# An adaptive-layer-norm block with a 4-bit gated network: the up product's first pass through seven block products as well

## The chip, the cores and the metric

The kernel runs on one core of a Trainium2 chip. The metric is the device time of one execution in microseconds, the median of three runs. Five engines run their own instruction streams in program order and meet through semaphores: TensorE (PE in the views), VectorE (DVE), ScalarE (ACT), GpSimd (POOL, idle here but for the start) and SyncE (SP), which issues every DMA.

## What is computed

```python
mod = (_silu(L0_c) @ L0_wmod).reshape(L0_c.shape[0], 6, 1, -1)      # sa, ca, ga, sb, cb, gb
h = _layernorm(x, axis=-1) * (1 + ca) + sa
x = x + ga * _L0_attn_ref(h, ...)          # h @ (masked 1024x1024 weight).T
h = _layernorm(x, axis=-1) * (1 + cb) + sb
x = x + gb * _L0_ffn_ref(h, ...)
# ffn: w1, w2 (2752x1024) and w3 (1024x2752) are 4-bit codes through a 16-entry table, times a scale per 64
h = jax.nn.silu(jnp.einsum('bsd,hd->bsh', x, w1)) * jnp.einsum('bsd,hd->bsh', x, w2)
return jnp.einsum('bsh,dh->bsd', h, w3)
```

x is 4 batches of 512 tokens by 1024, all float32. Two of the batches are called pass 0 here and the other two pass 1.

## The kernel before

**Numbers.** Each float32 operand of a product is split into a high and a low part (`_hi`, `_lo`, both in the format fp32r), and a product is three matmuls: high by high, high by low, low by high. Splitting costs a copy (the high part) and a subtraction (the low part). A 4-bit code becomes a weight in 8 chained Prelu activations on ACT (`lines`) and one multiplication with the scale on DVE.

**Stages.** First comes the attention product with both layer norms. Then the up product: hidden width 2752 is 21 tiles of 128 (numbered 0 to 20) and a half tile (FULL, 21). A tile has a gate part from w1 (w = 0) and an up part from w2 (w = 1). Then the down product, which is not changed here.

**Pass 0** is plain: `up_group(c, w, b)` is, for tile c, part w and batch b, 8 chunks of the inner dimension by 3 matmuls, so 24 matmuls of 128x128 by 512 columns into one of six PSUM banks, 96 for a tile. ACT does the `silu` of the w = 0 groups, DVE multiplies the two into h (`make_h`), SP stores h. Beside it ACT decodes tile c + 1 (`lines`, once for each w), DVE scales and splits it (`finish`), and DVE also forms five sums of halves of w1 and w2 (`sums`) which SP stores into the DRAM tensor `t_d`, for pass 1.

**Pass 1** computes the 2x2 blocks (gate and up, by batch) with seven block products in place of eight, each of 12 matmuls, 84 for a tile. The weight operands m1 to m7 come back from `t_d` (`load_stream`), are split again (`stream_high` on ACT, `stream_low` on DVE), and each product has a PSUM bank of its own. Sums and differences of the two batches' inputs (`x_add`, `x_high`, `x_low`) are made once, the last of them while pass 0 still runs. DVE adds the products up (`use_m1` to `use_m7`). ACT decodes w3 beside it.

**Order.** Nothing is scheduled by a program: each engine's list of calls is written out by hand, and an engine does exactly the next call, or waits. `load_codes` brings a tile's codes by DMA into a place that an earlier tile's raw weights held.

## Time and profile before

| | us |
|---|---|
| median of three runs | 1570.31 (1570.2 to 1570.99) |
| span of the profiled execution | 1567.6 |
| around the span, against the median | 2.7 |
| PE busy | 1539.4 |
| DVE busy | 1029.5 |
| ACT busy | 989.6 |

The span is from the first to the last instruction of one profiled execution. PE is the TensorE matmul stream. A single matmul is shown with 0.39 us since it is pipelined; how often one starts is read from the starts in the timeline.

### The profile page before, as it was taken

Reading aid. Unit: us, or ns where it says so; the run is one execution under the profiler, and the core shown is the slowest. Engines: PE = TensorE matmul, PEld = TensorE weight load, DVE = VectorE, ACT = ScalarE, POOL = GpSimd, SP = SyncE. Lnnn points to the kernel's source line nnn. Section 1 sums busy time; section 2 is a strip of 40 time slices with the busy share of each in tenths; the row PEclk is TensorE's granted clock in tenths of the full one; section 3 lists DMA queues with packets and bytes.
Section 4 is the critical chain, followed back from the end, with each engine's and each line's share of the span. In section 5 each row is a group of like instructions: output and inputs, shape, how many; then the busy total and the mean of one; then the engine's idle time right before and its main releaser. Section 6 shows DMA issues by size and latency. Waiting matters only on the chain.

```text
span 1567.6 us, 19154 instructions
## 1 busy us (share of the span) xinstructions
PE 1539.4 (98%) x7200; PEld 1269.6 (81%) x7200; DVE 1029.5 (66%) x1486; ACT 989.6 (63%) x1290; POOL 5.5 (0%) x10
## 2 busy tenths in 40 slices
PE   5899999999999999999999999999999999999999
PEld 3688888888888888888888888888888888888887
DVE  5687786555555455547676666666875757956994
ACT  3475676998888888884898988785433432333220
POOL 0000000000000000000000000000000000000000
PEclk9999999999999999999999999999999999999999
DMA  9976423564555445532778787786777868947973
GB/s 368 372 258 228 134 81 138 177 200 166 186 169 187 153 162 180 178 128 97 257 228 252 207 250 208 207 254 171 260 292 272 332 204 302 343 160 268 397 279 122
DMA packets 170139, 345.97 MB, mean 221 GB/s; under 512 B 14752, under 2 KB 65344, under 8 KB 170048
## 3 DMA queue, kind: packets, MB, share of 16 engines
q1 hardware_dynamic: 170048, 344.76, 65.1%
q8 instruction: 57, 0.93, 0.3%
q14 instruction: 34, 0.28, 0.1%
HBM read 249.77 MB, written 94.93 MB: 220 GB/s over the span
## 4 chain that ended last, share of the span: by engine, by line
PE 96%; DMA 2%; DVE 0%; ACT 0%; SPq 0%; issue 0%
PE ps L1916 10%; PE ps L1915 10%; PE ps L1914 10%; PE ps L1988 9%; PE ps L1987 9%; PE ps L1989 9%; PE ps L1925 9%; PE ps L1927 9%; PE ps L1926 9%; PE ps L1832 4%; PE ps L1834 4%; PE ps L1833 4%; DMA wmod<-wmod 2%; PE ps L1789 2%; PE ps L1772 1%; DVE attn_w_lo L1368 0%
## 5 line engine op out<-in xcount | busy, mean ns | idle before, releaser
L861 ACT ACTIVATE w_raw<-w_raw 128x1024 f32<-128x1024 f32 x287 | 304.6, 1061 | 9.1
L1914 PE MATMUL ps<-ffn_in_hi,w_hi 128*128 128x512 f32 x688 | 268.6, 390 | 0.0
L1916 PE MATMUL ps<-ffn_in_hi,w_lo 128*128 128x512 f32 x688 | 267.8, 389 | 0.0
L1915 PE MATMUL ps<-ffn_in_lo,w_hi 128*128 128x512 f32 x688 | 267.7, 389 | 0.0
L1987 PE MATMUL ps<-t_hi,s_hi 128*128 128x512 f32 x616 | 239.6, 389 | 0.0
L1988 PE MATMUL ps<-t_lo,s_hi 128*128 128x512 f32 x616 | 239.6, 389 | 0.0
L1989 PE MATMUL ps<-t_hi,s_lo 128*128 128x512 f32 x616 | 239.6, 389 | 0.0
L1925 PE MATMUL ps<-x_m_hi,stream_hi 128*128 128x512 f32 x604 | 235.0, 389 | 0.0
L1926 PE MATMUL ps<-x_m_lo,stream_hi 128*128 128x512 f32 x604 | 235.0, 389 | 0.0
L1927 PE MATMUL ps<-x_m_hi,stream_lo 128*128 128x512 f32 x604 | 235.0, 389 | 0.0
L1114 ACT ACTIVATE s_hi<-s_raw 128x1408 fp32r<-128x1408 f32 x56 | 77.4, 1383 | 241.2 <-DVE s_raw L1624 192.6
L873 ACT ACTIVATE w_raw<-w_raw 128x1024 f32<-128x1024 f32 (+1 forms) x154 | 163.4, 1061 | 4.4
L1172 DVE SCALAR_TENSOR_TENSOR w_raw<-w_raw,w_scale 128x1024 f32<-128x1024 f32 x41 | 50.3, 1226 | 174.4 <-ACT w_raw L861 174.4
L1916 PEld LDWEIGHTS ps<-ffn_in_hi,w_lo 128*128 128x128 f32 x688 | 129.1, 188 | 26.8
L1915 PEld LDWEIGHTS ps<-ffn_in_lo,w_hi 128*128 128x128 f32 x688 | 129.2, 188 | 26.6
L1914 PEld LDWEIGHTS ps<-ffn_in_hi,w_hi 128*128 128x128 f32 x688 | 129.2, 188 | 26.5
L1987 PEld LDWEIGHTS ps<-t_hi,s_hi 128*128 128x128 f32 x616 | 115.6, 188 | 24.1
L1989 PEld LDWEIGHTS ps<-t_hi,s_lo 128*128 128x128 f32 x616 | 115.6, 188 | 24.0
L1988 PEld LDWEIGHTS ps<-t_lo,s_hi 128*128 128x128 f32 x616 | 115.6, 188 | 23.9
L1927 PEld LDWEIGHTS ps<-x_m_hi,stream_lo 128*128 128x128 f32 x604 | 113.4, 188 | 23.6
L1926 PEld LDWEIGHTS ps<-x_m_lo,stream_hi 128*128 128x128 f32 x604 | 113.4, 188 | 23.6
L1925 PEld LDWEIGHTS ps<-x_m_hi,stream_hi 128*128 128x128 f32 x604 | 113.4, 188 | 23.4
(136 smaller groups left out, 2078.1 us busy)
## 6 DMA issues: line engine op xcount, KB each, us to landing
s_raw<-h_d SPq DMA_DIRECT2D x96, 704.0 KB, 5.6
stream_raw<-t_d SPq DMA_DIRECT2D x150, 256.0 KB, 3.4
t_d<-combined SPq DMA_DIRECT2D x106, 256.0 KB, 2.6
wmod<-wmod SPq DMA_DIRECT2D x12, 2048.0 KB, 15.3
t_raw<-w_d SPq DMA_DIRECT2D x88, 256.0 KB, 6.1
w_codes<-w12q SPq DMA_DIRECT2D x41, 512.0 KB, 5.3
h_d<-h_tile SPq DMA_DIRECT2D x44, 256.0 KB, 2.4
h_d<-up_c SPq DMA_DIRECT2D x44, 256.0 KB, 3.3
```

What stands on the lines that cost most here:

```text
L861: act.activation(RAWF[r], RAWF[r] if j else RQ[r][:], ACT.Prelu, bias=bias, scale=sign, alpha=slope).then_inc(line_ready, 1)
L873: act.activation(E3[p][0:rows, :], (E3 if j else E3Q)[p][0:rows, :], ACT.Prelu, bias=bias, scale=sign, alpha=slope).then_inc(w3_line, 1)
L1114: act.activation(SH[p][:], SR[p][:, 1], ACT.Copy).then_inc(s_hi, 1)
L1914: pe.matmul(acc, RH[r][:, k, :], HH[:, b, k, :], start=(k == 0), stop=False)
L1915: pe.matmul(acc, RH[r][:, k, :], HL[:, b, k, :], start=False, stop=False)
L1916: last = pe.matmul(acc, RL[r][:, k, :], HH[:, b, k, :], start=False, stop=(k == C - 1))
L1925: pe.matmul(acc, th[:, k, :], xh[:, k, :], start=(first and k == 0), stop=False)
L1926: pe.matmul(acc, th[:, k, :], xl[:, k, :], start=False, stop=False)
L1927: last = pe.matmul(acc, tl[:, k, :], xh[:, k, :], start=False, stop=(stop and k == HALF_C - 1))
L1987: pe.matmul(acc, SH[p][:, k, :], TH[place(i)][k][:], start=(k == 0), stop=False)
L1988: pe.matmul(acc, SH[p][:, k, :], TL[place(i)][k][:], start=False, stop=False)
L1989: last = pe.matmul(acc, SL[p][:, k, :], TH[place(i)][k][:], start=False, stop=(k == HC - 1))
```

## The change

Only tiles 0 to 2 of pass 0 stay plain (`PLAIN = 3`). Tiles 3 to 20 of pass 0 go through the seven block products too. A step g is one tile of one pass; g = 0 is tile 3 of pass 0, and g = 18 the first tile of pass 1.

- Products of a step now share three PSUM banks: m1, m2 and m5 open them, m4 goes onto m2's bank, m3 onto m5's, m7 and m6 onto the same two. They go onto a bank only when ACT or DVE has read what is in it: m4 waits for ACT's copy of m2, m3 for DVE's use of m5, m7 for the copy of m2 + m4, m6 for the silu of m5 + m3. m7 and m6 of a step come after m1, m2 and m5 of the next.
- Block weights have twelve places in SBUF, taken in turn. In pass 0 DVE writes the sums straight into them (`weight_sum`), and makes high and low parts (`split_up`); SP stores the sums to `t_d` out of them, and a low part, which takes the sum's place, waits for that store.
- The inputs of the ffn product go through a DRAM tensor `xm_d`: `store_modulated` after each tile of 128 tokens, `load_stage` as four pieces of 1 MB a pass. `x_sum`, `x_high` and `x_low` now exist for both passes. ACT's and DVE's next write of the modulated tile waits for the store of the one before.
- `lines(n)` decodes both parts of a tile in one activation of 128x2048, and is one tile further ahead.
- The transposes of pass 1's inputs move from plain tiles 1 to 8 to the steps of tiles 4 to 11.

The core of the diff:

```diff
+    PLAIN = 3
+    GROUPS = [(c, w, b) for c in range(PLAIN) for w, b in order0(c)]
...
+    OPEN, CLOSE, MIDDLE = ("m1", "m2", "m5"), ("m7", "m6"), ("m4", "m3")
+    STEPS_UP = [(0, c) for c in range(PLAIN, FULL)] + [(1, c) for c in range(FULL)]
+    LAST_STEP = [FULL - PLAIN - 1, len(STEPS_UP) - 1]
+    TAILS = [-1, -2]
     TAIL_PARTS = [("m2", "m2", 0), ("m4", "m4", 0), ("m2", "m5", 1), ("m3", "m3", 1)]
...
+    UP_PRODUCTS = with_ends(
+        lambda g: [(g, n) for n in OPEN] + [(g - 1, n) for n in CLOSE if has_previous(g)] + [(g, n) for n in MIDDLE],
+        lambda g, tail: [(tail, 0), (tail, 1), (g, "m7"), (g, "m6"), (tail, 2), (tail, 3)])
...
+    def up_bank(g, name):
+        return 2 + 3 * (g % 2) + {"m5": 0, "m3": 0, "m6": 0, "m2": 1, "m4": 1, "m7": 1, "m1": 2}[name]
...
+                    old = n - 2
+                    if old < PLAIN:
+                        sp.wait_ge(w12_lo, 2 * old + 2)
+                        sp.wait_ge(ts_added, len(SUM_NAMES) * (old + 1))
+                    else:
+                        sp.wait_ge(t_ready, READY.index((step_of(0, old), "m3" if w == 0 else "m4")) + 1)
+                        sp.wait_ge(sum_made, UP_SUMS.index((step_of(0, old), "m6")) + 1)
...
+            def store_modulated(e):
+                b, k = place2(e)
+                sp.wait_ge(modulated2, e + 1)
+                if e >= SHARED_FROM:
+                    sp.wait_ge(half_modulated, e - SHARED_FROM + 1)
+                for d in range(2):
+                    row = (2 * b + d) * P
+                    sp.dma_start(xm_d[row:row + P, :].rearrange("p (c t) -> p c t", c=HALF_C)[:, :, k * P:(k + 1) * P],
+                                 HM[hm_of(e)][:, HALF_C * d:HALF_C * (d + 1), :]).then_inc(xm_stored[hm_of(e)], 16)
+
+            def load_stage(pas, d, b):
+                row = (2 * (2 * pas + b) + d) * P
...
+            store_modulated(6)
             sp.wait_ge(gated, TILES)
             for w in range(2):
                 load_s12(1, w)
+            for w in range(2):
+                load_codes(2, w)
+            sp.wait_ge(xm_stored[1], xm_stores(6))
+            for d in range(2):
+                load_stage(0, d, 0)
+            for w in range(2):
+                store_part(0, w, w)
+            store_modulated(HALF_TILES - 1)
+            sp.wait_ge(xm_stored[1], xm_stores(HALF_TILES - 1))
+            for d in (1, 0):
+                load_stage(0, d, 1)
+            for name in SUM_NAMES:
+                store_sum(0, name)
+            for n in range(1, PLAIN):
+                for w in range(2):
+                    store_part(n, w, w)
+                    load_s12(n + 1, w)
+                for name in SUM_NAMES:
+                    store_sum(n, name)
+                if n == 2:
+                    load_codes(3, 0)
+                    load_codes(3, 1)
+                for b in range(2):
...
+            for d, b in ((0, 1), (1, 1), (0, 0), (1, 0)):
+                if (d, b) == (0, 0):
+                    sp.wait_ge(sum_made, len(UP_SUMS))
...
+                load_stage(1, d, b)
...
-            def lines(n, w, first=0, last=NL):
-
-                r, J = ring(n, w), job(n, w)
-                act.wait_ge(codes_loaded[r], 16 * ((n + 1) // 2))
+            def lines(n, first=0, last=NL):
+
+                cols = slice(0, C * P * (1 if n == FULL else 2))
+                act.wait_ge(codes_loaded[n % 2], code_loads(n))
...
-                        act.wait_ge(line_ready, NL * J + j)
-                    act.activation(RAWF[r], RAWF[r] if j else RQ[r][:], ACT.Prelu,
+                        act.wait_ge(line_ready, NL * (n - 1) + j)
+                    act.activation(RAW2[n % 2][:, cols], RAW2[n % 2][:, cols] if j else RQ2[n % 2][:, cols], ACT.Prelu,
                                    bias=bias, scale=sign, alpha=slope).then_inc(line_ready, 1)
...
+                        act.wait_ge(xm_stored[1], xm_stores(e - 1))
...
+            lines(1, 2)
+            silu(0, 0)
+            lines(2, 0, 3)
+            silu(0, 1)
+            lines(2, 3)
+            silu(1, 0)
+            for name in ("m1", "m4", "m3"):
+                x_high(0, name)
+            silu(1, 1)
+            lines(3)
+            silu(2, 0)
+            lines(4, 0, 3)
+            silu(2, 1)
+            lines(4, 3, 5)
+            x_high(0, "m7")
+            x_high(0, "m6")
+            lines(4, 5)
+            for c in range(PLAIN, FULL):
+                g, n = step_of(0, c), c + 2
+                if has_previous(g):
+                    copy_up(g - 1, "m4")
+                    silu_up(g - 1, 1)
+                if n <= FULL:
+                    lines(n, 0, 2)
+                copy_up(g, "m2")
+                if n <= FULL:
+                    lines(n, 2, 5)
+                if turned_in(c) is not None:
+                    input2(turned_in(c))
+                if has_previous(g):
+                    silu_up(g - 1, 0)
+                if n <= FULL:
+                    lines(n, 5)
+            g, tail = LAST_STEP[0], TAILS[0]
+            copy_up(g, "m4")
+            silu_up(g, 1)
+            x_high(1, "m1")
+            silu_up(tail, 0)
+            x_high(1, "m2")
+            silu_up(g, 0)
+            x_high(1, "m5")
+            x_high(1, "m4")
+            for name in OPEN:
+                weight_high_up(step_of(1, 0), name)
+            silu_up(tail, 1)
+            x_high(1, "m3")
+            for c in range(FULL):
...
+            def split_up(g, names):
+                for name in names:
+                    if (g, name) not in ACT_HI:
+                        weight_high_up(g, name)
+                for name in names:
+                    weight_low_up(g, name)
...
+            sums(0)
+            make_h(0, 0)
+            finish(1, 0)
+            finish(1, 1)
+            sums(1)
+            make_h(0, 1)
+            for name in ("m1", "m4", "m3", "m6", "m7"):
+                x_sum(0, name)
+            finish(2, 0)
+            finish(2, 1)
+            sums(2)
+            make_h(1, 0)
+            x_low(0, "m1")
+            make_h(1, 1)
+            x_low(0, "m4")
+            x_low(0, "m3")
+            combine(3, 0)
+            combine(3, 1)
+            for name in OPEN:
+                weight_sum(0, name)
+            split_up(0, OPEN + ("m4",))
+            make_h(2, 0)
+            make_h(2, 1)
+            split_up(0, ("m3",))
+            for name in CLOSE:
+                weight_sum(0, name)
+            x_low(0, "m7")
+            x_low(0, "m6")
+            split_up(0, CLOSE)
+            for c in range(PLAIN, FULL):
+                g, n = step_of(0, c), c + 1
+                nxt = step_of(0, n)
+                if n == FULL:
+                    combine(FULL, 0)
+                    weight_sum(nxt, "m2")
+                else:
+                    combine(n, 0)
+                    combine(n, 1)
+                    for name in OPEN + CLOSE:
+                        weight_sum(nxt, name)
+                    split_up(nxt, OPEN)
+                both_used(g)
+                first_left(g)
+                if turned_in(c) is not None:
+                    modulate_half(turned_in(c))
+                if has_previous(g):
+                    finish_c11(g - 1)
+                split_up(nxt, ("m4",))
+                if has_previous(g):
+                    finish_c22(g - 1)
+                split_up(nxt, ("m3",))
+                if has_previous(g):
+                    make_h_up(g - 1, 1)
+                split_up(nxt, ("m2",) if n == FULL else CLOSE)
+                if has_previous(g):
+                    make_h_up(g - 1, 0)
+
+            gl, tail, first = LAST_STEP[0], TAILS[0], step_of(1, 0)
+            x_sum(1, "m1")
+            x_low(1, "m1")
+            x_low(1, "m2")
+            finish_c11(gl)
+            make_h_up(tail, 0)
+            finish_c22(gl)
+            make_h_up(gl, 1)
+            make_h_up(gl, 0)
+            x_low(1, "m5")
+            x_sum(1, "m4")
+            split_up(first, OPEN)
+            make_h_up(tail, 1)
+            x_low(1, "m4")
+            x_sum(1, "m3")
             def w3_combine(j):
                 p, rows = j % 3, w3_rows(j)
                 dve.wait_ge(w3_line, NL * (j + 1))
@@ -1590,31 +1872,35 @@
...
+                elif name == "m4":
+                    pe.wait_ge(up_copied, 2 * g + 1)
+                elif name == "m3":
+                    pe.wait_ge(up_c_step, c_at(g, "e"))
+                elif name == "m7":
+                    pe.wait_ge(up_copied, 2 * g + 2)
+                elif name == "m6":
+                    pe.wait_ge(silu_done, gated_by(g, 1))
+                block_product(ps[:, up_bank(g, name), :], TT[slot_of(g, name)], x_operand(g, name), name in OPEN, True, name not in OPEN)
...
```

The first place is DVE between the first and the second plain tile. `w_raw` are decoded weights, `combined` the sums for pass 1, `h_tile` is h, `x_m_raw` a sum of two input blocks. Before:

```order
L1172 SCALAR_TENSOR_TENSOR w_raw_89<-w_raw_89,w_scale_93 128x1024 [waits s12_loaded_1,line_ready]
L1177 CAST w_hi_73<-w_raw_89 128x1024 [waits combined]
L1179 TENSOR_TENSOR w_lo_77<-w_raw_89,w_hi_73 128x1024 [waits w12_hi]
L1193 TENSOR_TENSOR combined_101<-w_raw_89 128x512
L1459 TENSOR_TENSOR h_tile_96<-silu_g_94,ps 128x512 [waits group_done,silu_done]
L1193 TENSOR_TENSOR combined_102<-w_raw_88,w_raw_89 128x512
L1193 TENSOR_TENSOR combined_103<-w_raw_89,w_raw_88 128x512
L1459 TENSOR_TENSOR h_tile_97<-silu_g_95,ps 128x512 [waits group_done,silu_done]
L1193 TENSOR_TENSOR combined_100<-w_raw_88,w_raw_89 128x512 [waits ts_stored_0]
L1172 SCALAR_TENSOR_TENSOR w_raw_86<-w_raw_86,w_scale_92 128x1024 [waits s12_loaded_0,line_ready]
L1177 CAST w_hi_70<-w_raw_86 128x1024 [waits combined,group_done]
L1179 TENSOR_TENSOR w_lo_74<-w_raw_86,w_hi_70 128x1024 [waits w12_hi]
```

After:

```order
L1742 TENSOR_TENSOR x_m_raw<-ffn_in_raw_00_153,ffn_in_raw_11_156 128x2048 [waits stage_loaded_11,stage_loaded_00]
L1742 TENSOR_TENSOR x_m_raw<-ffn_in_raw_10_154,ffn_in_raw_00_153 128x2048 [waits stage_loaded_00,stage_loaded_10]
L1742 TENSOR_TENSOR x_m_raw<-ffn_in_raw_01_155,ffn_in_raw_11_156 128x2048 [waits stage_loaded_11,stage_loaded_01]
L1742 TENSOR_TENSOR ffn_in_raw_01_155<-ffn_in_raw_00_153,ffn_in_raw_01_155 128x2048 [waits xs_added,stage_loaded_01,stage_loaded_00]
L1742 TENSOR_TENSOR ffn_in_raw_11_156<-ffn_in_raw_10_154,ffn_in_raw_11_156 128x2048 [waits xs_added,stage_loaded_11,stage_loaded_10]
L1379 SCALAR_TENSOR_TENSOR w_raw_80<-w_raw_80,w_scale_84 128x1024 [waits s12_loaded_0,line_ready]
L1388 CAST w_hi_66<-w_raw_80 128x1024 [waits combined,group_done]
L1390 TENSOR_TENSOR w_lo_70<-w_raw_80,w_hi_66 128x1024 [waits w12_hi]
L1379 SCALAR_TENSOR_TENSOR w_raw_80<-w_raw_80,w_scale_85 128x1024 [waits s12_loaded_1,line_ready]
L1388 CAST w_hi_67<-w_raw_80 128x1024 [waits combined,group_done]
L1390 TENSOR_TENSOR w_lo_71<-w_raw_80,w_hi_67 128x1024 [waits w12_hi]
L1410 TENSOR_TENSOR combined_94<-w_raw_80 128x512 [waits ts_stored_2,combined]
```

The five sums of inputs now stand ahead of the scaling and splitting of tile 2 (rows with `w_scale`), which the third plain tile on PE waits for.

The second place is SP between the sums of two tiles; `w_codes` are the DMAs that bring codes. Before:

```order
L587 DMA t_d<-combined_102 128x512 [waits ts_added]
L587 DMA t_d<-combined_103 128x512 [waits ts_added]
L594 DMA h_d<-h_tile_97 128x4x128 [waits h_made]
L587 DMA t_d<-combined_100 128x512 [waits ts_added]
L463 DMA w_codes_84<-w12q 128x1024 [waits pure_stored_2,ts_added,w12_lo]
L463 DMA w_codes_85<-w12q 128x1024 [waits pure_stored_3,ts_added,w12_lo]
L469 DMA w_scale_92<-w12s 128x1x128 [waits combined]
L582 DMA t_d<-w_raw_86 128x512 [waits combined]
```

After:

```order
L711 DMA t_d<-w_raw_80 128x512 [waits combined]
L580 DMA w_scale_85<-w12s 128x1x128 [waits combined]
L717 DMA t_d<-combined_94 128x512 [waits ts_added]
L717 DMA t_d<-combined_95 128x512 [waits ts_added]
L717 DMA t_d<-combined_92 128x512 [waits ts_added]
L717 DMA t_d<-combined_93 128x512 [waits ts_added]
L717 DMA t_d<-combined_94 128x512 [waits ts_added]
L574 DMA w_codes_79<-w12q 128x1024 [waits pure_stored_2,ts_added,w12_lo]
L574 DMA w_codes_79<-w12q 128x1024 [waits pure_stored_3,ts_added,w12_lo]
L736 DMA h_d<-h_tile_88 128x4x128 [waits h_made]
L736 DMA h_d<-h_tile_89 128x4x128 [waits h_made]
```

The codes of tile 3 (`w_codes_79`, before `w_codes_84` and `_85`) are now issued behind the last stored sum of tile 2; before, behind the last of tile 1.

The third place is DVE at the end of pass 0. `up_left_then_c` and `up_c` are results of the block products, `up_weight_lo` the low parts of pass 1's first weights; before, `stream_lo` are those. Before:

```order
L1464 TENSOR_TENSOR x_m_raw<-ffn_in_raw_51,ffn_in_raw_54 128x2048 [waits group_done]
L1455 MEMSET h_tile_96 64x512 [waits h0_stored_0,group_done,silu_done]
L1459 TENSOR_TENSOR h_tile_96<-silu_g_94,ps 64x512
L1464 TENSOR_TENSOR x_m_raw<-ffn_in_raw_53,ffn_in_raw_51 128x2048
L1474 TENSOR_TENSOR x_m_lo<-x_m_raw,x_m_hi 128x2048 [waits xc_hi] x2
L1507 TENSOR_TENSOR stream_lo<-stream_raw,stream_hi 128x512 [waits tt_hi] x5
L1464 TENSOR_TENSOR ffn_in_raw_53<-ffn_in_raw_53,ffn_in_raw_54 128x2048
L1459 TENSOR_TENSOR h_tile_97<-silu_g_95,ps 128x512 [waits h0_stored_1,group_done,silu_done]
L1464 TENSOR_TENSOR x_m_raw<-ffn_in_raw_51,ffn_in_raw_52 128x2048 [waits group_done]
L1464 TENSOR_TENSOR x_m_raw<-ffn_in_raw_52,ffn_in_raw_54 128x2048
L1474 TENSOR_TENSOR x_m_lo<-x_m_raw,x_m_hi 128x2048 [waits xc_hi]
```

After:

```order
L1742 TENSOR_TENSOR x_m_raw<-ffn_in_raw_00_157,ffn_in_raw_11_160 128x2048 [waits up_m_done,stage_loaded_11,stage_loaded_00]
L1748 TENSOR_TENSOR x_m_lo<-x_m_raw,x_m_hi 128x2048 [waits xc_hi]
L1748 TENSOR_TENSOR x_m_lo<-ffn_in_raw_00_157,x_m_hi 128x2048 [waits xc_hi]
L1751 TENSOR_TENSOR up_gate_164<-ps,up_left_then_c_1_162 128x512 [waits h_made,up_c_step,up_m_done]
L1785 MEMSET up_left_then_c_0_161 64x512 [waits h_stored_0,silu_done]
L1786 TENSOR_TENSOR up_left_then_c_0_161<-up_left_then_c_0_161,ps 64x512
L1751 TENSOR_TENSOR up_left_then_c_1_162<-ps,up_left_then_c_1_162 128x512 [waits up_c_step,up_m_done]
L1789 TENSOR_TENSOR up_left_then_c_1_162<-up_gate_165,up_left_then_c_1_162 128x512 [waits up_c_step,silu_done]
L1792 TENSOR_TENSOR up_c_163<-up_gate_164,up_c_163 128x512 [waits up_copied,silu_done]
L1748 TENSOR_TENSOR x_m_lo<-ffn_in_raw_11_160,x_m_hi 128x2048 [waits xc_hi]
L1742 TENSOR_TENSOR x_m_raw<-ffn_in_raw_10_158,ffn_in_raw_00_157 128x2048 [waits up_m_done,stage_loaded_00,stage_loaded_10]
L1457 TENSOR_TENSOR up_weight_lo<-up_weight_raw,up_weight_hi 128x512 [waits act_hi] x3
```

Pass 1's first weights now have their low parts made behind three blocks' low parts (`x_m_lo`) and two sums (`x_m_raw`), the last two of these behind results of pass 0.

## Rows read from the trace of the kernel before

**Rows 1.** The page: span, shares of the engines, TensorE's clock and the chain of waits.

```profile
span 1567.6 us, 19154 instructions
PE 1539.4 (98%) x7200; PEld 1269.6 (81%) x7200; DVE 1029.5 (66%) x1486; ACT 989.6 (63%) x1290; POOL 5.5 (0%) x10
PEclk9999999999999999999999999999999999999999
PE 96%; DMA 2%; DVE 0%; ACT 0%; SPq 0%; issue 0%
```

**Rows 2.** PE's timeline (start us, us, engine, line, operation): three stages' first matmuls.

```profile
256.98 0.48 PE L1914 MATMUL ps<-ffn_in_hi,w_hi 128*128 128x512 f32 x1
...
733.94 0.39 PE L1925 MATMUL ps<-x_m_hi,stream_hi 128*128 128x512 f32 x1
...
1144.66 0.39 PE L1987 MATMUL ps<-t_hi,s_hi 128*128 128x512 f32 x1
```

**Rows 3.** Busy us by stretch: PE, PEld, DVE, ACT, POOL; then PEclk, DMA share, GB/s.

```profile
500.00:600.00 100.00, 100.00 (x443) 82.78 (x442) 57.49 (x68) 80.64 (x82) 0.00 (x0) 1.00 0.53 173
```

**Rows 4.** ACT's timeline around the start of the plain groups.

```profile
264.39 1.49 ACT L906 ACTIVATE modulated<-ps,mod 128x128 f32<-128x128 f32 x4
265.91 1.06 ACT L950 ACTIVATE ffn_in_hi<-modulated 128x1024 fp32r<-128x1024 f32 x1
...
272.31 1.28 ACT L1033 ACT_TABLE_LOAD   x1
...
275.19 7.62 ACT L861 ACTIVATE w_raw<-w_raw 128x1024 f32<-128x1024 f32 x7
```

**Rows 5.** DVE's timeline of the same stretch.

```profile
262.22 0.82 DVE L1340 TENSOR_SCALAR normed_again<-x,mean_var,rstd_fine 128x1024 f32<-128x1024 f32 x1
...
268.15 2.35 DVE L1182 TENSOR_TENSOR w_raw_first<-w_hi,w_lo 128x1024 f32<-128x1024 f32 x2
272.33 1.23 DVE L1172 SCALAR_TENSOR_TENSOR w_raw<-w_raw,w_scale 128x1024 f32<-128x1024 f32 x1 [1.82 <-ACT w_raw L861]
...
274.31 1.23 DVE L1179 TENSOR_TENSOR w_lo<-w_raw,w_hi 128x1024 fp32r<-128x1024 f32 x1
...
287.17 1.28 DVE L1193 TENSOR_TENSOR combined<-w_raw,w_raw 128x512 f32<-128x512 f32 x2
```

**Rows 6.** Groups of instructions: busy us, mean ns of one, idle before.

```profile
L1048 ACT ACTIVATE x_m_hi<-x_m_raw 128x2048 fp32r<-128x2048 f32 x4 | 7.7, 1916 | 11.1 <-DVE x_m_raw L1464 11.1
...
L1066 ACT ACTIVATE up_c<-ps 128x512 f32<-128x512 f32 x42 | 24.7, 588 | 13.7 <-PE ps L1927 13.7
...
L1172 DVE SCALAR_TENSOR_TENSOR w_raw<-w_raw,w_scale 128x1024 f32<-128x1024 f32 x41 | 50.3, 1226 | 174.4 <-ACT w_raw L861 174.4
...
L1177 DVE CAST w_hi<-w_raw 128x1024 fp32r<-128x1024 f32 x41 | 28.5, 694 | 4.4 <-DVE w_raw L1172 0.5
...
L1464 DVE TENSOR_TENSOR x_m_raw<-ffn_in_raw,ffn_in_raw 128x2048 f32<-128x2048 f32 x4 | 9.1, 2287 | 3.6 <-PE ps L1916 3.5
...
L1624 DVE TENSOR_TENSOR s_raw<-s_raw 128x1408 f32<-128x1408 f32 x40 | 64.8, 1620 | 24.1 <-DMA s_raw<-h_d 24.1
```

**Rows 7.** DMA: GB/s in 40 slices; KB each and us to landing; w_codes' extremes.

```profile
GB/s 368 372 258 228 134 81 138 177 200 166 186 169 187 153 162 180 178 128 97 257 228 252 207 250 208 207 254 171 260 292 272 332 204 302 343 160 268 397 279 122
...
t_d<-combined SPq DMA_DIRECT2D x106, 256.0 KB, 2.6
...
w_codes<-w12q SPq DMA_DIRECT2D x41, 512.0 KB, 5.3
h_d<-h_tile SPq DMA_DIRECT2D x44, 256.0 KB, 2.4
h_d<-up_c SPq DMA_DIRECT2D x44, 256.0 KB, 3.3
...
DMA to landing us min/median/max: 3.5/5.2/9.2
```

**Rows 8.** Waits by engine and line: ACT on a store of h.

```profile
ACT s_hi L1114 <- DMA h_d<-up_c: 5.9, 1, 5.9
```

999 lines of the change are left out of this document (530 added, 469 removed).

## The prediction

> **What bounds the kernel now.** I read the page first: PE is busy 1539.4 of 1567.6 us, its clock row shows 9 (full speed, 2.4 GHz) in every slice, and 96% of the chain of waits is PE [rows 1]. So PE's matmuls set the time. In a stretch inside pass 0, PE is busy 100.00 of 100 us, ACT 80.64 and DVE 57.49 [rows 3]. The price of a matmul I take from starts, not from the 0.39 us shown: pass 1 has 21 x 84 + 48 = 1812 matmuls between 733.94 and 1144.66 [rows 2], so 410.72 / 1812 = 0.2267 us each, with no room for waits. The plain stage runs from 256.98 to 733.94: 86 groups of 24, 2064 x 0.2267 = 467.8, leaves 9.1 us for nine times eight transposes, 1.01 each time. So PE waits nowhere from 257 on, and whatever waits the change brings are all loss.
>
> A block product is 12 x 0.2267 = 2.72 us, a plain group 5.44, a plain tile 21.76, a step of seven products 19.04.
>
> **What is saved.** 18 tiles of pass 0 go from 96 to 84 matmuls; the half tile keeps 48. 216 x 0.2267 = 49.0 us.
>
> **Can the other engines keep a step of 19.04 us?** ACT: a chained line of 1024 takes 7.62 / 7 = 1.09 [rows 4] at a mean of 1.06; no row shows a line of 2048, but a copy of that size takes 1.92 [rows 6], so I take 1.95 (bounds: 1.92, and 2 x 1.09 = 2.18). Eight are 15.6, four copies and silus at 0.5 (0.588 each, the next one starting before the end [rows 6]) 2.0: 17.6, and 19.1 in the eight tiles with a modulation of 1.5 [rows 4], where PE has 20.05. DVE: two scalings 2.3, five sums at 0.6 (1.28 for two, the ends overlap [rows 5]) 3.0, seven high parts at 0.35 (0.694 for twice the size [rows 6]) 2.5, seven low parts 4.2, six results at 0.6 3.6, and half a us of chained gaps: 16.1, or 17.4. Both fit. What PE waits for is ready at least 5 us early once a step runs (ACT's copy of m2 ends 8.5 us into the step, m4 wants it at 13.6), so I put nothing on a step.
>
> **The start, step by step,** on the old clock. Here the order decides.
> (a) The last modulated tile may be written only when the one before is stored. SP issues that after the layer norm's last step, 262.22 + 0.82 = 263.04 [rows 5]; two stores at 2.4 to 3.3 each [rows 7] land at about 266.5, where ACT had begun at 264.39 [rows 4]. Modulation 1.5, copy 1.0, low part 1.2: 270.4. PE wants it at 256.98 + 10.88 + 1.01 = 268.9. Wait 1.5 (0.5 to 3).
> (b) ACT then does the last six lines of tile 1, 11.7, a table load 1.28 [rows 4] and a silu: 282.6. DVE's first five sums stand ahead of that h: they wait for the last modulated tile's store (behind the restored weights, 270.4 + 2.35 [rows 5], landing 277), and the fifth waits for the first one's store, issued at 278.1 behind two loads of 1 MB. At 372 GB/s, the second slice of the page [rows 7], 2.1 MB are 5.7 us: 285. Then h, and scaling and splitting of tile 1, 274.31 + 1.23 - 272.33 = 3.2 [rows 5]: 289.5. PE is through tile 0 at 281.3. Wait 8.2 (5.1 if nothing queues: then 286.4 by the silu).
> (c) PE does tile 1 to 311.3. DVE splits the second part (292.6), makes five sums with one wait for a store (296.8), h (297.4), then five sums of inputs at 2.2 (2.287 [rows 6]): 308.4, and tile 2 at 311.6. Wait 0.3. PE does tile 2 to 333.4.
> (d) DVE's second part and sums end at 318.9. Only then does SP issue tile 3's codes (the second place in the change); landing 5.3 [rows 7]: 325.0. ACT has been free since 314.6. Eight lines: 340.5. Scalings, three sums, four high parts and one low part, 6.8: 347.3. Wait 13.9 (9 to 16).
> (e) m1, m2 and m5 end at 355.5. m4 wants ACT's copy of m2, which stands behind two silus, the eight lines of tile 4, two high parts of inputs (3.65) and two lines of tile 5: 340.5 + 24.7 = 365.2. Wait 9.7.
> (f) m3 wants DVE's use of m5, behind scaling, sums and six parts of tile 4: 360.8 + 8.9 = 369.7, against m4's end 367.9. Wait 1.8.
> Together 35.4 (26 to 41).
>
> **Between the passes.** Count from the start of the last step of pass 0; PE needs 13 products, so it is through at 35.4. SP's four loads of 1 MB for pass 1 stand behind the last store of h in its queue, about 18.2; the third, which the first sum needs, lands with 3.7 MB ahead and in it at 372 GB/s at about 29.1. DVE: sum 31.4, ACT high 33.3, DVE low of m1 35.6 and m2 38.0, two results, the half tile's h with a fill of 0.5, two h: 41.6; low of m5 43.8, sum for m4 46.1; ACT high 48.1 and weights 48.7; first weight's low part 49.4. PE waits 14.0. Without the loads' queue it is 6.9, since m5's input place is free only at 32.6 and the same chain follows. In the next 20 us: m4 waits for a copy of m2 behind m3's input, 2.8; m3 for its input 0.9; the next m1 for its weights behind two sums and a split 4.4. Together 22.1 (15 to 25).
>
> **The end of pass 1.** The last 1408-wide sum and split (1.62 each [rows 6]) now stand behind results that end with m6, 5.4 us before PE is through. The first low part is ready 2.5 after, the second after a silu and h of the half tile 3.0 later than wanted: 5.5 (0 to 8).
>
> **The sum.** -49.0 + 35.4 + 22.1 + 5.5 = +14.0 us, on the profiled execution's 1567.6 + 2.7 around it, which is the median 1570.3: **1584.3**.
>
> **Rivals.**
> *Transfers land at their quickest, and it ends level.* For: codes have landed in 3.5 [rows 7], and pass 0 moves only 173 GB/s on average [rows 3]. Against: at these places loads of 1 MB are issued together. Price: (a) -0.9, (b) -3.1, the store waits in (c) and (d) -2.3, codes -1.7, between the passes -7.1: 14.0 - 15.1 = -1.1, so 1569.2, not slower. It decides when the third load of pass 1 lands within 4 us of its issue.
> *The waits are mostly hidden.* For: both helpers have idle time in pass 0 [rows 3], and if the codes of tile 3 and the inputs' sums do not hold each other up, the start costs about 10 and the middle 8. Against: every step above is an order in the code. 1570.3 - 49.0 + 18 = 1539.
> *A loop through the store of h holds every step.* ACT's copy into the single place `up_c` waits for the store of the step before, which waits for DVE's last h, which waits through scaling for ACT's lines. Round it goes L + 17.6 + 16.1 in two steps, L the store with its issue: at 3.4 that is 18.6, below 19.04; from 4.4 on it decides, and one wait for such a store was 5.9 [rows 8]. At 6.0 a step is 19.9, and 21.3 in the eight with modulation: 10 x 0.8 + 8 x 1.3 = 18, less the 5 that are in hand: +13, 1597.
> The Trainium skill ("DMA: Bandwidth & Descriptors", section on the anatomy of one DMA) gives 2.0 us plus bytes / 436 GB/s for a transfer of the GpSimd path: by it codes would land in 3.2 where the row has 5.3, and the third load in 9.2 where I have 10.9; the sum would be some 4 us less. It bears on the first rival; the row for 256 KB (2.6) agrees with it and the one for 512 KB does not. Its section on queues and rings says that each DMA engine consumes its descriptors in ring order; by that the small store in (b) does stand behind the two loads, and otherwise the sum would be 3.1 less. No run here shows it yet.
>
> **How the numbers follow.** My forecast 0.60, with its own range 1575 to 1594; quick transfers 0.15; hidden waits 0.10; the loop 0.13; something else 0.02. The range 1563 to 1601 takes in the forecast with its bounds (26 + 15 + 0 - 49 = -8 to 41 + 25 + 8 - 49 = +25, 1562 to 1595), the first rival and the loop, and leaves out the second. A measurement of this kernel can tell 0.2%, 3.1 us, from no change. Faster by more: 0.10, half of quick transfers 0.05, 0.01 of the rest: 0.16. Within: half of quick transfers 0.08 and a low tail of the forecast 0.04: 0.12. Slower: 0.72.
>
> **What would show it.** PE idle: some 8 us before the second plain tile, 14 before the first m1, 10 before the first m4, 14 before pass 1's first m1; next to nothing inside a step. ACT idle 10 us before its eight lines of tile 3, released by a DMA of codes. Pass 1's first matmul near 734, where it is now, though the work ahead of it is 49 us less. The forecast is wrong if PE's idle time from 257 on is below 52 us, or if steps of pass 0 take over 19.3 us (20.3 with transposes).

## The result, and the profile after

The changed kernel takes 1631.88 us (median of four runs, 1624.84 to 1635.37) against 1570.26: a ratio of 1.0387, with a 95% interval of 1.0363 to 1.0410. I had forecast slower, by 14 us; it is slower by 61.6, outside my range. The profiled execution spans 1629.8 us (1567.6 before), so 49.0 us of matmuls went and 111 us came. The page of the changed kernel, against [rows 1]:

```profile
span 1629.8 us, 19234 instructions
...
PE 1516.3 (93%) x6984; PEld 1242.1 (76%) x6984; DVE 1128.8 (69%) x1750; ACT 938.8 (58%) x1089; POOL 5.5 (0%) x10
...
PEclk9999999889999999997999999999999999999999
...
PE 39%; DMA 7%; DVE 4%; issue 2%; ACT 1%; SPq 1%; DVEq 0%; ACTq 0%
```

The 216 matmuls are gone, and PE's share fell with them: 98 to 93%. Its clock row, all 9 before, now has 8s and a 7. The timeline of PE shows where it waited; the bracket is the idle time ahead of a matmul and what ended it:

```profile
273.00 0.50 PE L2194 MATMUL ps<-ffn_in_hi,w_hi 128*128 128x512 f32 x1 [0.87 <-DVE ffn_in_lo L1580]
297.29 0.77 PE L2194 MATMUL ps<-ffn_in_hi,w_hi 128*128 128x512 f32 x1 [13.11 <-DVE w_lo L1390]
...
356.34 0.77 PE L2205 MATMUL ps<-x_m_hi,up_weight_hi 128*128 128x512 f32 x1 [13.17 <-DVE h_tile L1730]
...
370.80 0.76 PE L2205 MATMUL ps<-x_m_hi,up_weight_hi 128*128 128x512 f32 x1 [4.40 <-ACT up_left_then_c L1233]
...
478.40 0.77 PE L2205 MATMUL ps<-x_m_hi,up_weight_hi 128*128 128x512 f32 x1 [4.54 <-ACT up_c L1233]
...
767.07 0.79 PE L2205 MATMUL ps<-x_m_hi,up_weight_hi 128*128 128x512 f32 x1 [14.49 <-DVE up_weight_lo L1457]
...
1083.46 0.76 PE L2205 MATMUL ps<-x_m_hi,up_weight_hi 128*128 128x512 f32 x1 [2.34 <-DVE up_left_then_c L1751]
...
1203.49 0.79 PE L2278 MATMUL ps<-t_hi,s_hi 128*128 128x512 f32 x1 [4.23 <-DVE s_lo L1915]
```

From the starts of all matmuls behind 257 I add what each lies later than 0.2267 us (eight transposes: 1.01) behind the one ahead of it. That is a wait and whatever ran slowly behind it, and it can be laid beside the terms of the prediction. The sums hang a little on where a stage is cut and on how the transposes are counted; another count of the same starts gives up to 2 us more or less in a row.

| Place (us) | predicted | changed kernel | with all orders of calls changed, e10 |
|---|---|---|---|
| start, 257 to 377: (a) to (f) | 35.4 | 42.0 | 19.5 |
| inside the steps of pass 0 | 0 | 24.5 | 0 |
| between the passes | 22.1 | 24.3 | 10.7 |
| inside pass 1 | 0 | 11.2 | 0 |
| end of pass 1 | 5.5 | 7.7 | 2.4 |
| sum | 63.0 | 109.7 | 32.6 |

Three things are in the second column that were not in the first: the steps of pass 0, those of pass 1, and slow matmuls. In pass 0 all six waits of PE lie between 430 and 572, in the eight steps that have transposes; from 572 to 720 PE waits nowhere. Waits of ACT from 377 to 720 (us in total, times, longest), which answer to [rows 8]:

```profile
ACT up_c L1233 <- DMA h_d<-up_c: 48.7, 13, 5.9
ACT up_gate L1250 <- DVE up_gate L1751: 3.8, 1, 3.8
```

And one turn of that wait. SP's queue, then the end of DVE's h, then ACT:

```profile
465.37 1.24 SPq L665 DMA_DIRECT2D xm_d<-modulated  x2
466.66 0.64 SPq L656 DMA_DIRECT2D normed_back<-xn_d  x1
467.41 0.96 SPq L574 DMA_DIRECT2D w_codes<-w12q  x2
468.43 0.43 SPq L742 DMA_DIRECT2D h_d<-up_left_then_c  x1
468.90 1.22 SPq L742 DMA_DIRECT2D h_d<-up_c  x1
```

```profile
466.82 0.68 DVE L1792 TENSOR_TENSOR up_c<-up_gate,up_c 128x512 f32<-128x512 f32 x1
```

```profile
477.66 0.60 ACT L1233 ACTIVATE up_c<-ps 128x512 f32<-128x512 f32 x1 [5.95 <-DMA h_d<-up_c]
```

h is made at 467.50 and its place is free at 477.66: L, the store with its issue, is 10.2 us. Two stores of modulated tiles, a load of normed rows and 1 MB of codes stand ahead of it, 2 MB in all. In [rows 7] a store of h took 2.4 to 3.3 (medians). Over seven turns, from the h of 420.1 to that of 561.8, L is 7.3 to 10.2, 8.9 on the mean.

### The profile page after: what moved, and what is told of

Its sections match the earlier page's. It is cut to its first block, busy times and chain, and to the rows that moved or that the text cites. A ratio compares the mean times of both kernels' runs of the same rounds, so it can differ in the third digit from the quotient of the medians.

```text
span 1629.8 us, 19234 instructions
## 1 busy us (share of the span) xinstructions
PE 1516.3 (93%) x6984; PEld 1242.1 (76%) x6984; DVE 1128.8 (69%) x1750; ACT 938.8 (58%) x1089; POOL 5.5 (0%) x10
## 4 chain that ended last, share of the span: by engine, by line
PE 39%; DMA 7%; DVE 4%; issue 2%; ACT 1%; SPq 1%; DVEq 0%; ACTq 0%
PE ps L2278 8%; PE ps L2279 8%; PE ps L2280 8%; PE ps L2205 5%; PE ps L2206 5%; PE ps L2207 5%; DMA h_d<-up_c 2%; DMA w_scale<-w3s 2%; DMA up_weight_raw<-t_d 2%; DMA w_d<-w_raw 1%; DVE up_weight_lo L1457 1%; DVE up_left_then_c L1751 1%; DVE w_raw L1873 1%; DMA ffn_in_raw<-xm_d 1%; DVE x_m_raw L1742 1%
## 5 line engine op out<-in xcount | busy, mean ns | idle before, releaser
L2205 PE MATMUL ps<-x_m_hi,up_weight_hi 128*128 128x512 f32 x972 | 387.2, 398 | 62.2 <-DVE up_weight_lo L1457 18.3
L2206 PE MATMUL ps<-x_m_lo,up_weight_hi 128*128 128x512 f32 x972 | 385.2, 396 | 0.0
L2207 PE MATMUL ps<-x_m_hi,up_weight_lo 128*128 128x512 f32 x972 | 384.6, 396 | 0.0
L1030 ACT ACTIVATE w_raw<-w_raw 128x2048 f32<-128x2048 f32 (+1 forms) x147 | 275.4, 1874 | 3.6
L2205 PEld LDWEIGHTS ps<-x_m_hi,up_weight_hi 128*128 128x128 f32 x972 | 186.8, 192 | 107.4 <-issue 34.6
L2207 PEld LDWEIGHTS ps<-x_m_hi,up_weight_lo 128*128 128x128 f32 x972 | 186.7, 192 | 39.8
L2206 PEld LDWEIGHTS ps<-x_m_lo,up_weight_hi 128*128 128x128 f32 x972 | 186.5, 192 | 38.7
L1457 DVE TENSOR_TENSOR up_weight_lo<-up_weight_raw,up_weight_hi 128x512 fp32r<-128x512 f32 x241 | 154.9, 686 | 60.0 <-ACT up_weight_hi L1227 51.2
L2111 PE MATMUL ps<-attn_w_hi,attn_in_hi 128*128 128x512 f32 x256 | 102.1, 399 | 1.9 <-DVE attn_in_lo L1549 1.9
L2113 PE MATMUL ps<-attn_w_hi,attn_in_lo 128*128 128x512 f32 x256 | 100.2, 391 | 0.0
```

What stands on the lines that cost most here:

```text
L1030: act.activation(RAW2[n % 2][:, cols], RAW2[n % 2][:, cols] if j else RQ2[n % 2][:, cols], ACT.Prelu, bias=bias, scale=sign, alpha=slope). ...
L1457: dve.tensor_tensor(TT[i][1], src, TT[i][0].bitcast(F32), ALU.subtract).then_inc(t_ready, 1)
L2111: pe.matmul(acc, AH[par][:, c, :], WH[:, c, cols], start=(c == 0), stop=False)
L2113: last = pe.matmul(acc, AL[par][:, c, :], WH[:, c, cols], start=False, stop=(c == C - 1))
L2205: pe.matmul(acc, th[:, k, :], xh[:, k, :], start=(first and k == 0), stop=False, skip_group_check=onto)
L2206: pe.matmul(acc, th[:, k, :], xl[:, k, :], start=False, stop=False, skip_group_check=onto)
```

## Experiments

All but g1, which starts from the kernel before, start from the changed kernel. Each is measured against the kernel before on its own chip; "us off" is against 1631.88. The changed kernel's own times lie 10.5 apart, so a few us of a difference are no result by themselves; where the traces say at which place PE lost less, it is given.

**g1_gaps: what a wait costs beside itself.**

```diff
+            for k, (c, n) in enumerate(GAPS):
+                pool.wait_ge(group_done, 4 * c)
+                for _ in range(n):
+                    pool.memset(GROUP[:], 0.0).then_inc(gap_over, 1)
...
+                if (w, b) == (0, 0) and c in [q for q, _ in GAPS]:
+                    pe.wait_ge(gap_over, sum(n for q, n in GAPS if q <= c))
```

> The kernel before, with six idle stretches of PE between plain tiles 5|6, 7|8, 9|10, 11|12, 13|14 and 15|16: PE waits for a chain of 3, 5, 7, 11, 20 and 40 small writes on GpSimd, each some 0.3 us, into constants no longer used. Theory A (an idle stretch of over 2 us drops TensorE to half its clock, and the matmuls behind it run at that for a few us): the matmuls behind the longer stretches start 0.42 us apart and not 0.227 for some 9 of them, 2 us lost each time on top of the stretch, nothing behind the shortest; the loss does not grow from 6 to 12 us. Theory B (the slow matmuls in the changed kernel come from its traffic or its shapes): every matmul behind a stretch starts 0.227 us after the one before.

Measured: 1604.19, 34.7 us above its kernel before. PE's timeline behind the second and the fourth stretch:

```profile
444.40 0.50 PE L1925 MATMUL ps<-ffn_in_hi,w_hi 128*128 128x512 f32 x1 [1.43 <-POOL four_partition_groups L846]
444.74 0.40 PE L1926 MATMUL ps<-ffn_in_lo,w_hi 128*128 128x512 f32 x1
444.97 0.39 PE L1927 MATMUL ps<-ffn_in_hi,w_lo 128*128 128x512 f32 x1
...
539.51 0.79 PE L1925 MATMUL ps<-ffn_in_hi,w_hi 128*128 128x512 f32 x1 [3.01 <-POOL four_partition_groups L846]
540.10 0.63 PE L1926 MATMUL ps<-ffn_in_lo,w_hi 128*128 128x512 f32 x1
540.53 0.63 PE L1927 MATMUL ps<-ffn_in_hi,w_lo 128*128 128x512 f32 x1
```

and the stretches behind the fourth (length; busy time of PE, PEld, DVE, ACT, POOL; granted clock, DMA share, GB/s):

```profile
539.40:541.60 2.20, 2.09 (x5) 1.71 (x6) 2.06 (x3) 0.00 (x0) 0.06 (x1) 0.50 1.01 307
542.70:580.00 37.30, 37.30 (x166) 30.88 (x165) 15.81 (x18) 29.14 (x30) 0.00 (x0) 1.00 0.36 119
```

Waits of 0.85, 1.43, 1.96, 3.01, 5.82 and 11.16 us cost 1.1, 1.7, 3.8, 4.7, 7.6 and 13.7: 0.3 on top for the first two, 1.7 to 2.5 for the others, with matmuls 0.43 apart at a granted clock of 0.50 (1.2 GHz) for some 8. Theory A holds: the cost beside the wait is 1.9, 1.7, 1.8 and 2.5, so it does not grow in step with the wait. The changed kernel has eleven such places, about 23 of its 110 us. Theory A's "over 2 us" does not hold, though: 1.96 was enough here, and the length alone does not decide. Behind 268 us, in all traces of this case, no wait under 1.8 us is followed by a row of slow matmuls and each of the 52 waits of 3.6 us or more is; between these, a wait of 1.81 (e4, at 376) is, and waits of 2.90 (e5, at 507) and 3.52 (e6, at 377) are not. What decides there no run shows.

**e6_fill: can that be had back?**

```diff
+            def fill(bank, count):
+                for _ in range(count):
+                    pe.matmul(ps[:, bank, :], HH[:, 0, 0, 0:P], HH[:, 0, 0, :], start=True, stop=True)
...
+                    if g == 4:
+                        fill(4, 50)
...
```

> Edit: PE fills three of its waits with matmuls of data at hand into a bank that nothing reads: 50 (11.3 us) before the second plain tile, 50 before the first m1 of pass 0, 13 (2.9 us) before the first m4. Nothing else changes. Theory A (what follows a wait at half the clock costs 2.3 + 1.9 + 3.1 us at these three): the waits become shorter than 2 us, the matmuls behind them run at full pace, and the time falls by 6 to 1626 (1623 to 1628.5). Theory B (the slow matmuls come from what else goes on there): nothing falls, 1631 to 1634.

Measured: 1627.15, 4.7 us off, with intervals that overlap (1.0341 to 1.0387 of the kernel before, against 1.0363 to 1.0410). The slow matmuls behind 297 and 371 are gone; those behind 356 stay, since 3.74 us of that wait were left. But a new wait came for m3, which had been ready just in time:

```profile
377.05 0.47 PE L2211 MATMUL ps<-x_m_hi,up_weight_hi 128*128 128x512 f32 x1 [3.52 <-DVE up_left_then_c L1751]
```

Counted from the first plain matmul, e6 is 3.1 us ahead at the start of the third plain tile, 1.2 at the first m1 and nothing at the second step's first m1 (122.1 us, in the changed kernel 122.0). All that PE won there it waited out again. The 4.7 us lie behind it, at places that the edit does not touch. So theory A is right on the pace and wrong on the time: the slow clock's 23 us are an upper bound of its price, and these fillings had nothing back.

**e1_h_first: the store of h ahead of the codes.**

```diff
                 if e is not None:
                     store_modulated(e)
-                    if e + 2 < TILES:
-                        load_normed(e + 2 - HALF_TILES)
-                codes_after(c + 1)
                 if has_previous(g):
                     for b in (1, 0):
                         store_h_up(g - 1, b)
+                if e is not None and e + 2 < TILES:
+                    load_normed(e + 2 - HALF_TILES)
+                codes_after(c + 1)
```

> Edit: in pass 0 SP issues the two stores of h (1 step back) ahead of the load of normed rows and of the two loads of codes, not behind them. Theory A (the store of h holds the step: made at 467.5, landed at 477.7, because 1.5 MB of loads and stores are ahead of it): the store lands in 3 to 4 us, ACT's copy of m4 into up_c waits for no store in pass 0, PE's six waits on that copy between 430 and 571 (17.2 us, 24.5 with the slow matmuls behind them) go; but the codes are then issued some 1.3 us later and land when ACT wants them, so a third of it comes back as a wait for codes. Forecast 1616 us (1608 to 1622). Theory B (the transfers' total decides, and only the name of the late one changes): the codes land 4 us too late in place of the store, steps stay at 23 to 24 us, and the time at 1627 to 1633.

Measured: 1615.33, 16.5 us off, as A has it. ACT's waits in the same stretch:

```profile
ACT w_raw L1030 <- DMA w_codes<-w12q: 38.7, 15, 5.8
ACT up_gate L1250 <- DVE up_gate L1751: 7.2, 2, 4.4
ACT up_c L1233 <- DMA h_d<-up_c: 5.9, 3, 4.4
```

and the landing of the stores of h there, of the changed kernel (first) and of e1:

```profile
DMA to landing us min/median/max: 2.3/5.9/8.7
```

```profile
DMA to landing us min/median/max: 2.3/2.5/4.3
```

Theory A holds with its second half: the same bytes in another order, the store of h lands in 2.5, and the codes become the next loop. In the step shown above they are now issued at 468.48, behind the store, though DVE has left their place at 463.90, and ACT waits 3.60 for them. By place, the steps of pass 0 lose about 15 us, where the six traces that keep the old order there lose 20 to 26: 5 to 11 us are the edit's own, and 4 to 5 of the rest lie in pass 1, which it leaves alone. By the Trainium skill ("DMA: Bandwidth & Descriptors", section on queues and rings) each DMA engine consumes its descriptors in ring order; the two medians agree.

**e2_w3_last: pass 1.**

```diff
                     finish_c11(g - 1)
-                for j in w3_ended(c - 1)[1:]:
-                    w3_combine(j)
-                if has_previous(g):
                     finish_c22(g - 1)
                     make_h_up(g - 1, 1)
                     make_h_up(g - 1, 0)
+                for j in w3_ended(c - 1)[1:]:
+                    w3_combine(j)
```

> Edit: in pass 1 DVE scales the second w3 tile of a step behind the results of m6 and both h, not ahead of m6's result. Theory A (the results stand behind a wait of some 6 us for the scale of w3): PE's waits on up_left_then_c at 887, 946, 1024, 1083 and 1144 (with their slow matmuls 10.3 us) go, the time is 1621.5 (1618 to 1625). Theory B (the m6 result is late because ACT's copies wait for the store of h): these waits stay, 1630 to 1634.

Measured: 1622.63, 9.3 us off, the number of A. In the changed kernel DVE stood 6.5 us for a scale of w3, with PE's result behind it:

```profile
885.06 1.23 DVE L1873 SCALAR_TENSOR_TENSOR w_raw<-w_raw,w_scale 128x1024 f32<-128x1024 f32 x1 [6.51 <-DMA w_scale<-w3s]
886.20 0.68 DVE L1751 TENSOR_TENSOR up_left_then_c<-ps,up_left_then_c 128x512 f32<-128x512 f32 x1
```

In e2's trace no wait of PE in pass 1 is released by that result. Five others are left, of 0.15 to 1.53 us, four of them for ACT's copy behind a store of h; inside pass 1 it loses 5.2, not 11.2. That these waits go is shown; their price is less than the 6.0, since the five other single runs from e1 to e6, which keep pass 1 as it was, lose only 6.7 to 8.0 there. Why the changed kernel's trace has 11.2 is open. The rest of its gain is mostly in pass 0, where the edit changes nothing: the loop's waits differ by a few us from run to run.

**e3_start and e5_start2: the start.** The calls of DVE in e3, and what e5 puts ahead besides:

```diff
-            sums(0)
-            make_h(0, 0)
             finish(1, 0)
+            make_h(0, 0)
             finish(1, 1)
-            sums(1)
+            sums(0)
             make_h(0, 1)
-            for name in ("m1", "m4", "m3", "m6", "m7"):
+            sums(1)
+            for name in ("m1", "m4", "m3"):
                 x_sum(0, name)
...
+            both_used(0)
+            first_left(0)
             x_low(0, "m7")
```

> Edit: only the order of calls from the first plain tile to the first step of seven products: DVE finishes tile 1 before the first sums and makes the inputs' sums around tile 2; SP loads the codes of tile 3 once tile 1 is stored; ACT decodes tile 3 before the high parts of the inputs and copies m2 of the first step before the end of tile 4. Theory A (order, not speed, makes the 42 us that PE lost from 262 to 377): ACT begins tile 3 near 304 instead of 331, the first m1 starts near 330 instead of 356, the second step's first m1 near 352 instead of 377, and the time falls by 25 to 1607 (1600 to 1613). Theory B (the transfers that stand in a row at the start make it, 5 MB between 265 and 285): the waits move to other places and at most 10 us go, 1622 or more.

Measured: 1623.04, 8.8 us off, not 25: the number of theory B, but not its cause, for the start did move. ACT began tile 3 at 305.98, tile 1 of PE waited 2.04 and not 13.11, but a new wait took the place:

```profile
371.22 0.76 PE L2211 MATMUL ps<-x_m_hi,up_weight_hi 128*128 128x512 f32 x1 [20.09 <-DVE up_left_then_c L1755]
```

My theory had missed that DVE adds m5 (`both_used`, for m3) behind its work on tile 4. Hence:

> Edit: e3_start with three calls more put forward: ACT copies m2 of the first step once PE can be through with it and not 9 us before, DVE adds m5 and m1 of that step before it works on tile 4, and SP issues the loads of normed rows behind the weights' stores. Theory A (e3 fell short since the result of m5 stood behind tile 4, which kept m3 for 20 us): m3's wait goes, the first m1 of the second step starts near 357 instead of 377 in the changed kernel and in e3, and the time is 1612 (1606 to 1618). Theory B (ACT's decoding rate sets the second step): it starts at 365 or later, 1620 or more.

Measured: 1606.97, 24.9 us off. The second step's first m1 starts at 356.98, as forecast; the start loses 20.6 us, of which 12.6 in one place, before that m1. Its weights come behind ACT's decoding of tile 4, which ends at 349.26, and behind DVE's own work, which keeps it busy up to the scaling at 349.73: one is as late as the other.

**e4_boundary: between the passes.**

```diff
+                if c == FULL - 1:
+                    for i in range(2):
+                        sp.wait_ge(xm_stored[i], xm_stores(TILES - 2 + i))
+                    for d in range(2):
+                        load_stage(1, d, 1)
                 weights_io(step_of(0, c + 1), c + 1)
...
```

> Edit: between the passes only. SP loads the two x blocks whose places are long free one step earlier and the other two as soon as the places of the last decoded tiles are free, ahead of the last stores of h in its queue; DVE splits the half tile's weights before it waits for PE's results, and the first weights of pass 1 right behind the inputs of m1 and m2; ACT likewise. Theory A (the order puts the third load at 746 and with it everything to 767): that load lands near 733, the first matmul of pass 1 is no longer kept (14.5 us and 3 of slow matmuls), of the two waits behind it half stays, and the time falls by 18 to 1614 (1608 to 1620). Theory B (the loads are slow for the traffic that is under way with them): loads issued earlier land later than 740 and delay the stores of h with them; 1624 or more.

Measured: 1615.99, 15.9 us off. Pass 1's first m1 no longer waits; between the passes 14.5 us are lost and not 24.3, the first m4 now waits 6.24 for ACT's copy of m2, which stood behind two inputs. So 10 us come from the place itself and the rest, as in e2, from the steps' own spread: right in time, half right in the account.

**e7_all: the four together.** e1, e2, e4 and e5.

> Edit: e4, e5, e2, and e1 with the load of normed rows behind the codes. If the four are independent places, their gains add: 18 + 20 + 9 + 17 us off 1632, 1568 (1558 to 1578), level with the kernel before. If the transfers or ACT's lines are what is short in pass 0, the start's gain is eaten by the steps behind it and it stays above 1580.

Measured: 1585.53, 46.4 us off, where 66.6 single ones add up to. By place it lost 22.3, 10.5, 13.4, 3.2 and 11.5. The start, the middle and pass 1 are near those of the single runs. So it stayed above 1580, the rival's number. What does not add is for the most part spread that each single run had and counted as its own. Taken at its own place, against the mean of the traces that leave this place alone, e5 is worth about 21 us, e1 8, e4 10 and e2 3, some 41 in all. Against that the end of pass 1 is 3.8 worse: ACT stood 12.3 us at 1100 for a store of h that SP issued late, and copied m2 late.

**e8_orders to e11_orders2_fill: the rest.** Of e8, at the end of pass 1; of e10, in a step of pass 0:

```diff
             split_up(tail, TAIL_NAMES)
+            s_add(0)
             t_units(0, range(4))
+            s_low(0)
             finish_c11(gl)
```

```diff
-                    for name in OPEN + CLOSE:
+                    for name in OPEN:
                         weight_sum(nxt, name)
-                    split_up(nxt, OPEN)
+                    for name in OPEN:
+                        weight_high_up(nxt, name)
...
+                if n < FULL:
+                    for name in OPEN:
+                        weight_low_up(nxt, name)
```

> Edit: e7 with more calls put in another order, none added or taken away. Start: sums of tile 2 ahead of the last two input sums, codes of tile 4 ahead of the stores of h. Pass 0: the half modulation behind both h, its store and the load of normed rows behind the codes. Between: the first copy of m2 and the weights of m4 and m3 ahead of m3's input. Pass 1: the stores of h two loads earlier; the first loads of the down product behind the step's weights. End: the first input of the down product is summed and split before the last results of the up product. If PE's waits of e7 are each the order around them (12.7 at 359, 10.5 in pass 0, 12.3 at 738 and 748, 3.8 at 1110, 7.7 at 1157): -3, -5, -5, -4, -6, so 1562 (1553 to 1572), faster than the kernel before. If ACT's and DVE's work is what is short there, at most the last two go: 1575 or more.

Measured: 1568.88, 63.0 us off; against its kernel before 0.9991 (0.9980 to 1.0001), level and not yet faster. The end fell from 11.5 to 2.0 and pass 1 to nothing, as expected; the middle stayed at 13.8 and pass 0 at 11.6, where DVE's low parts waited 2.2 to 4.5 us, in six steps, for the stores of their own sums.

> Edit: e8, and the high parts of the inputs of m7 and m6 (two copies of 128 x 2048 in the first step) are made by GpSimd, which has nothing to do, and no more by ACT. If ACT's decoding of tile 4 sets the start of the second step (it ends at 351.1 in e7, DVE's first weight at 358.8), that start comes 3.7 us earlier than in e8 and the time is 3.7 less, 1558. Rival: GpSimd's copies take 5 us or more each, or slow DVE down, and the second step waits for the inputs of m7 in place of it: no less than e8.

Measured: 1572.81: the rival. ACT's lines of tile 4 ended hardly sooner (347.2 for 347.5), as it stood 1.9 us for PE's m2 in between. They did not decide either: DVE came to the scaling of tile 4 at 351.80, 4.6 us behind them, and in e8 too it was busy right up to it, at 347.70. Of these 4.1 us DVE was 1.6 late before; the others are two slow operations while GpSimd, which needed 8.89 us for the two copies, was at work. DVE's timeline of e9, then the same two in e8:

```profile
339.17 1.52 DVE L1468 CAST up_weight_hi<-w_raw 128x512 fp32r<-128x512 f32 x1
340.73 2.27 DVE L1478 TENSOR_TENSOR up_weight_lo<-w_raw,up_weight_hi 128x512 fp32r<-128x512 f32 x1
```

```profile
337.54 0.42 DVE L1466 CAST up_weight_hi<-w_raw 128x512 fp32r<-128x512 f32 x1
337.99 0.69 DVE L1476 TENSOR_TENSOR up_weight_lo<-w_raw,up_weight_hi 128x512 fp32r<-128x512 f32 x1
```

> Edit: e8 with three calls in another order. In pass 0 DVE makes the first three sums and high parts, the last two sums, adds m5 and m1 of the step before, and only then the low parts, which in e8 waited 2.9 to 3.4 us for the stores of their sums; and both h stand ahead of the last two splits, so that the codes behind them are issued 1.9 us earlier. Between the passes m4's input is summed while DVE waits for m1's. If the chain through DVE and the codes' landing still sets the steps of pass 0: half of its 14 us and 2 to 5 between the passes go, 1560 (1555 to 1565). If PE's remaining waits there come from the transfers alone: 1566 to 1570.

Measured: 1554.13 (1553.79 to 1554.67), 0.9902 of the kernel before (0.9886 to 0.9919): 15.5 us faster than the kernel before, and 6 more than I had expected, since the steps of pass 0 lose nothing any more, where I had expected half. DVE's waits there (372 to 700) for the stores of its sums fell from 29.1 us in e8 to 7.2. A stretch inside pass 0, in the columns of [rows 3], of the changed kernel and then of e10:

```profile
500.00:600.00 100.00, 90.74 (x394) 74.40 (x393) 76.92 (x137) 83.60 (x68) 0.00 (x0) 0.97 0.56 183
```

```profile
500.00:600.00 100.00, 100.00 (x446) 82.96 (x446) 85.89 (x148) 92.09 (x69) 0.00 (x0) 1.00 0.60 204
```

The same instructions in another order: PE, which did 394 matmuls in this stretch, does 446 and waits nowhere from 380 to 700.

> Edit: e10 and filling matmuls of data at hand into a bank that nothing reads, 34 (7.7 us) before the second step's first m1, 8 (1.8 us) before the first m3 and 7 (1.6 us) before the second m1 of pass 1. By g1 and e6 a wait that is cut below 2 us leaves no slow matmuls: 3 to 5 us off e10, 1556. If e10's waits there are already shorter than the filling, it adds up to 3 us instead.

Measured: 1553.68 (1553.07 to 1555.59), no different from e10. The slow matmuls are gone (4.9 us at two places), but behind the second of them the next wait, for DVE's `up_weight_lo`, ends 6.83 us later in both kernels: DVE sets it, and the slow matmuls had cost nothing there. Of what PE won at the first place, about 1 us is left when pass 0 ends.

## Why the prediction was wrong, point by point

- **What bounds the kernel, and the saving: right.** 216 matmuls and 49.0 us are gone.
- **(a) to (f): the mechanism right but for the last link of (d), sizes off both ways.** (a) was 4.0 for 1.5, (b) 15.4 for 8.2, (c) nothing for 0.3, (d) 15.0 for 13.9, (e) 7.5 for 9.7, (f) nothing for 1.8. In (b) I had the last modulated tile's store landed at 277 and the first sum's at 285; they landed at 283.5 and 292.7. e3 shows that the order of calls made it: the same wait is then 2.04. In (d) ACT's 9.67 us for the codes came as forecast, but the first m1 waited last for tile 2's h, which frees its bank and stands behind four low parts in DVE's list; I had it wait for the first of the low parts. The 29.1 for the third load does not follow from its own terms, 3.7 MB at 372 GB/s behind 18.2, which give 28.1 to 28.6, and the 9.2 that the prediction sets beside its 10.9 is, by the formula that it gives, the time of 3 MB. Neither is what went wrong.
- **"What PE waits for is ready at least 5 us early once a step runs ..., so I put nothing on a step": this step failed.** I had added up what ACT and DVE do in a step and found room (that was right, e10 runs it with PE full), and read the room as if no result travelled from one step to the next. It does, through the place `up_c`. The rival with that loop had the right mechanism and formula. With L = 8.9, the mean, it gives (8.9 + 19.1 + 17.4) / 2 = 22.7 us for a step with transposes; seven of ACT's copies, 429.75 to 570.46, are 23.5 apart. (Over 20.3 was the sign that I had set for being wrong.) In the steps without them, for which the rival had 8 us, the loop cost nothing: there a store of h landed in 4.3 (median) and not in 7.2. Its size was wrong, since I took L from medians of the old kernel, 3.3 in [rows 7] and at most 5.9 in [rows 8], where no megabyte of codes stood ahead of the store. Even there the longest of these stores took 7.3 (the view of L600 in the kernel before: `DMA to landing us min/median/max: 2.3/3.3/7.3`). The new order of SP was in the diff. I counted its queue at the start and between the passes, and not here.
- **Pass 1 at 0: failed.** DVE's queue held the last result of a step behind a load (e2), and what is left without that, 5.2, is mostly ACT's copy behind a store of h again.
- **Between the passes: right.** 24.3 for 22.1; the wait for m1 17.4 with its slow matmuls, for 14.0. That pass 1 would begin near 734 was wrong by 33 us, because of all the loss ahead of it.
- **The end: right**, 7.7 for 5.5.
- **"Whatever waits the change brings are all loss": too little.** Eleven of the waits also halved the clock behind them, for 1.7 to 2.5 us each time in g1, up to 23 us in all. How much of that the time would give back is open: at the places that were filled (e6) it gave back nothing.
- **The size.** 24.5 and 11.2 for nothing are 35.7 of the 46.7 us that are missing; the terms that I had, 74.0 for 63.0, are the other 11, with the clock in both. The range's upper end, 1601, had the loop at +13.

## What to carry to other kernels

When the sum of each engine's work in a step fits, look next for every place with one copy that is written in one step and freed by a transfer in another, and take the transfer's time with all that the new order puts ahead of it in the queue, not from the old kernel's median. A small store that frees a place goes ahead of large loads; work that can wait (a scale from DRAM, a low part whose raw data is being stored) goes behind results that PE waits for. Here the order of the calls alone, at all these places, was worth 78 us, and turned a change that saved work and lost 4% into one that wins 1%.
